# First attention layer of a two-layer network on one core: scores of a head pair interleaved by row halves, value matmuls on 256 queries, a second buffer for V

## The chip, the core and the metric

One core of a Trainium2 chip runs the whole program. The core has five engines that run their own queues and meet at semaphores: TensorE (matmuls and transposes, output into PSUM, eight banks of 512 f32 columns on 128 partitions), VectorE, ScalarE, GpSimd (POOL) and SyncE, which only issues DMAs here. The metric is the time of one execution in microseconds (us); less is better. Data are f32 unless a row says bf16. An f32 matmul instruction shows as two records (PE) and two weight loads (PEld) in the trace, a transpose as one of each.

## The reference, cut to what matters

The network is four residual blocks on x of shape (2, 1024, 128): an attention without projection of its output, a mixture of experts, a second attention with 16 heads, and a two-layer block with local attention. The change touches the first:

```python
    def _L0_attn_ref(x, Wq, Wk, Wv):
        ...
        Q = (x @ Wq.T).reshape(b, n, H, R)
        K = (x @ Wk.T).reshape(b, n, H, R)
        V = (x @ Wv.T).reshape(b, n, H, d)
        attn = jnp.einsum('bnhr,bmhr->bhnm', Q, K)
        attn = jax.nn.softmax(attn, axis=-1)
        out = jnp.einsum('bhnm,bmhd->bnd', attn, V)
        return out
    ...
    x = L0_attn_x
    x = x + _layernorm(_L0_attn_ref(_layernorm(x, axis=-1), L0_attn_Wq, L0_attn_Wk, L0_attn_Wv), axis=-1)
```

With H = 8 heads, R = 64 and d = 128: for each batch half and head, 1024 queries against 1024 keys, a softmax without scale or mask, and the weighted values summed over the heads.

## The kernel before

The first attention runs as four head pairs (`PAIRS`) times two batch halves: eight rounds, each of the same instructions. Heads of a pair lie side by side in the partitions: `q_st` and `k_st` hold head 0 on rows 0-63 and head 1 on rows 64-127; `v_st` holds the values of both, 128 columns each. A round has 16 units (`NU`): unit u is head u // 8 and the block of 128 queries u % 8.

For each unit TensorE makes the scores (`scores`, L557: two matmuls of 64 rows and 512 columns, into the bank pair 2 * (u % 2)), VectorE the negated maximum (L1115), ScalarE the exp with the row sum (L1557), VectorE one over the sum and the normalisation in place (L1120, L1122). TensorE transposes the probabilities by eight 128 x 128 transposes into banks 4 and 5 (`turn`, L572); ScalarE copies bank 4 (L1563) and VectorE bank 5 (L1128) into `probsT`. When the four units of a chunk (512 queries of one head) are there, eight matmuls with the values as weights and 512 columns add them into bank 6 or 7 (`weigh`, L582), two per unit, so that a chunk takes four units. Head 1 adds to what head 0 left in the bank, and VectorE adds the bank to `yT` (L1135).

What sets the order is the code of each engine's loop alone. On TensorE (L597 to L603): scores of u, transposes of u - 2, two value matmuls. The scores of u wait until the exp of u - 2 has freed its two banks. At the end of a round the projections of the next round stand between the last units: q (banks 0 and 1), k (2 and 3), and, last of all, V into banks 0 to 3 (`a_proj_v`), which ScalarE (L1541) and VectorE (L1101) copy into `v_st`. That buffer is single, so the V projection stands behind all value matmuls of the round. Unit 0 of the next round waits for q, k and the first half of V, unit 1 for the second half.

`probs` has four buffers (`NPB`), `probsT` two. GpSimd only copies the next pair's weights (L1785 to L1787). No DMA runs in this stage.

Of the kernel before, what the change touches and what calls it, by code (L numbers as in the profile page):

```python
# [12 lines left out]
P = 128  # L13
# [5 lines left out]
CH = 512  # L19
NCH = TOK // CH  # L20
# [35 lines left out]
def build(nc, a, out):  # L56
    with ExitStack() as ctx:
# [24 lines left out]
        probsT = sb("probsT", [P, 2, QT, CH])  # L82
        negmax = sb("negmax", [P, 2 * STRIP])
# [62 lines left out]
        v_nat = sb("v_nat", [P, TILES, P])  # L146

# [335 lines left out]
        def _(pe):  # L483
# [68 lines left out]
            with pe.Fori(0, PAIRS) as p:  # L552
                for b in range(BATCH):
# [3 lines left out]
                    def scores(u):  # L557
                        r, qt = R0 * (u // QT), u % QT
                        if u == 0:
# [3 lines left out]
                        elif u == 1:  # L563
                            pe.wait_ge(s_a_v1, m + 1)
                        else:
                            pe.wait_ge(s_a_exp, n0 + u - 1)
                        for n in range(2):
                            ins = pe.matmul(ps[:, 2 * (u % 2) + n, :], q_st[r:r + R0, qt * P:(qt + 1) * P],  # L568
                                            k_st[r:r + R0, n * CH:(n + 1) * CH], start=True, stop=True)
                        ins.then_inc(s_a_scores, 1)  # L570
# [11 lines left out]
                    def weigh(c, k0, k1):  # L582

                        head, qc = c // 2, c % 2
                        if k0 == 0:
                            pe.wait_ge(s_a_evA, n0 + 4 * c + 5)
                            pe.wait_ge(s_a_evB, n0 + 4 * c + 5)
                            if head == 0:
                                pe.wait_ge(s_a_oadd, 2 * m + 1)
                        for kt in range(k0, k1):  # L590
                            ins = pe.matmul(ps[:, 6 + qc, :], v_st[:, kt, head * P:(head + 1) * P],  # L591
                                            probsT[:, c % 2, kt, :], start=(head == 0 and kt == 0),
                                            stop=(head == 1 and kt == QT - 1), skip_group_check=True)
                        if head == 1 and k1 == QT:
                            ins.then_inc(s_a_pv, 1)

                    for u in range(NU):  # L597
                        scores(u)
                        if u >= 2:
                            turn(u - 2)  # L600
                        if u >= 6:
                            c, k = (u - 6) // 4, (u - 6) % 4
                            weigh(c, 2 * k, 2 * k + 2)  # L603
# [6 lines left out]
                    weigh(2, 4, 6)  # L610
                    pe.wait_ge(s_a_exp, n0 + NU)
                    a_proj_k(nb)
                    turn(NU - 1)
                    weigh(2, 6, 8)
                    weigh(3, 0, 8)
# [1357 lines left out]
```

## Time and profile before

| | us |
|---|---|
| median of 3 runs | 2117.53 |
| lowest and highest | 2064.26, 2120.01 |
| the profiled execution, its span | 2081.0 |
| TensorE busy in it (matmuls) | 1778.6 |
| VectorE, ScalarE, GpSimd busy | 1214.5, 927.3, 375.6 |

The profiled execution is one of its own and not among the three runs. In the rows below, a time is in us from the start of the span and a mean in ns; "x8" is the number of records in a merged row, and the time of a merged row runs from the start of its first record to the end of its last. Records overlap, since the next matmul begins while the last one still drains; for the pace one reads starts, not lengths. What stands in brackets is the idle time of the engine before the row and what ended it. PEclk or the mean clock is the granted share of 2.4 GHz; each short stretch is at 1.00 or 0.50.

### The profile page before, as it was taken

What the parts mean: (1) busy time and instruction counts of PE and PEld (TensorE: products, weight loads), DVE (VectorE), ACT (ScalarE), POOL (GpSimd) and SP (SyncE); (2) the same over time, 40 slices, a digit from 0 to 9 for tenths busy, and PEclk for the clock granted to TensorE, in tenths of its full rate; (3) what the DMA queues carried; (4) which work ended last, traced back from release to release, by engine and by line L of the source; (5) the groups of instructions that cost most, each with busy time, mean ns of one, the idle gap of its engine ahead of it and who ended that gap; (6) DMA issues with size and microseconds to landing.
All of it is one profiled execution on the core that took longest, in us unless ns stands there. A gap on an engine that the chain in (4) does not pass through costs nothing.

```text
span 2081.0 us, 31701 instructions
## 1 busy us (share of the span) xinstructions
PE 1778.6 (85%) x10724; PEld 954.1 (46%) x10724; DVE 1214.5 (58%) x2711; ACT 927.3 (45%) x2162; POOL 375.6 (18%) x208
## 2 busy tenths in 40 slices
PE   7999999999999879964999989989947886778766
PEld 4454444444544443332544545445524554245543
DVE  6554645546555546673665556546577764467744
ACT  2333423334333223322766657657525564255632
POOL 0000000000000002331000000000017873078820
PEclk8899988999999979985876668678778998889978
DMA  4000000000000000012000000000010000000000
GB/s 106 0 1 0 0 0 0 0 0 0 0 0 0 0 0 0 0 56 86 18 14 14 22 23 11 12 23 2 2 46 1 0 1 1 1 1 0 1 1 20
DMA packets 25961, 24.10 MB, mean 12 GB/s; under 512 B 4834, under 2 KB 19500, under 8 KB 25804
## 3 DMA queue, kind: packets, MB, share of 16 engines
q1 hardware_dynamic: 25836, 22.52, 3.6%
q8 instruction: 68, 1.11, 0.2%
q14 instruction: 57, 0.47, 0.1%
HBM read 18.32 MB, written 4.19 MB: 11 GB/s over the span
## 4 chain that ended last, share of the span: by engine, by line
PE 66%; POOL 12%; DVE 10%; issue 8%; ACT 2%; SPq 1%; DMA 1%; POOLq 0%; DVEq 0%; ACTq 0%
PE ps L568 12%; PE ps L591 11%; PE ps L796 7%; PE ps L578 7%; PE ps L740 5%; PE ps L766 5%; POOL ss L1862 4%; POOL probsT L1873 3%; PE ps L758 2%; DVE arena L1291 2%; PE ps L700 2%; POOL q_st L1860 2%; PE ps L804 2%; PE ps L694 1%; PE ps L541 1%
## 5 line engine op out<-in xcount | busy, mean ns | idle before, releaser
L1291 DVE CUSTOM_DVE_ANT_0 arena<-ps,arena 128x128 f32<-128x128 f32 (+7 forms) x258 | 194.2, 753 | 210.8 <-PE ps L740 161.1
L568 PE MATMUL ps<-k_st,q_st 64*128 64x512 f32 x512 | 269.0, 650 | 6.7 <-ACT probs L1557 6.7
L1115 DVE TENSOR_REDUCE negmax<-ps 128x1 f32<-128x1024 f32 x128 | 156.7, 1224 | 194.8 <-PE ps L568 194.8
L591 PE MATMUL ps<-probsT,v_st 128*128 128x512 f32 x512 | 238.7, 599 | 0.0
L1654 ACT ACTIVATE probs<-arena,negmax 128x128 f32<-128x128 f32 (+7 forms) x258 | 199.8, 775 | 57.9 <-DVE negmax L1294 54.9
L1563 ACT COPY probsT<-ps 128x512 f32<-128x512 f32 x128 | 74.9, 585 | 307.3 <-PE ps L578 307.3
L796 PE MATMUL ps<-ident,probs 128*128 128x128 f32 x832 | 190.6, 355 | 7.6 <-ACT probsT L1680 3.2
L1680 ACT COPY probsT<-ps 128x512 f32<-128x512 f32 (+3 forms) x256 | 127.2, 497 | 132.9 <-PE ps L796 132.2
L1557 ACT ACTIVATE probs<-ps,negmax 128x1024 f32<-128x1024 f32 x128 | 142.6, 1114 | 51.9 <-DVE negmax L1115 50.9
L578 PEld LDWEIGHTS ps<-ident,probs 128*128 128x128 f32 x1024 | 118.0, 147 | 100.8 <-issue 76.1
L796 PEld LDWEIGHTS ps<-ident,probs 128*128 128x128 f32 x832 | 113.9, 175 | 101.0 <-issue 87.3
L568 PEld LDWEIGHTS ps<-k_st,q_st 64*128 64x128 f32 x512 | 90.9, 196 | 149.6 <-issue 81.3
L578 PE MATMUL ps<-ident,probs 128*128 128x128 f32 x1024 | 147.7, 290 | 0.0
L1743 ACT ACTIVATE probsT<-ps,d_nm 128x128 f32<-128x128 f32 x256 | 89.9, 377 | 98.9 <-DVE d_nm L1450 98.9
L766 PE MATMUL ps<-probsT,v_st 128*32 128x128 f32 x2368 | 128.6, 327 | 5.1 <-issue 4.3
L591 PEld LDWEIGHTS ps<-probsT,v_st 128*128 128x128 f32 x512 | 90.9, 193 | 77.6 <-issue 77.6
L1785 POOL COPY wq_st<-w0qk 128x128 f32 (+1 forms) x5 | 1.5, 292 | 633.0 <-PE ps L568 613.4
L882 PE MATMUL ps<-arena 128*128 128x512 f32 x128 | 83.7, 790 | 35.0 <-ACT arena L1759 18.2
L1122 DVE TENSOR_SCALAR probs<-probs,rrow 128x1024 f32<-128x1024 f32 x128 | 96.4, 753 | 4.5
L740 PE MATMUL ps<-k_st,q_st 64*128 64x512 bf16 (+3 forms) x194 | 65.1, 393 | 36.6 <-DMA k_st<-c_parts 25.9
L1128 DVE COPY probsT<-ps 128x512 f32<-128x512 f32 x128 | 87.5, 684 | 14.3 <-PE ps L578 14.3
L1862 POOL TENSOR_TENSOR ss<-ss,half_c 128x16 f32<-128x16 f32 x32 | 93.2, 2912 | 0.4
(243 smaller groups left out, 2969.7 us busy)
## 6 DMA issues: line engine op xcount, KB each, us to landing
c_parts<-arena SPq DMA_DIRECT2D x4, 768.0 KB, 4.3
yT<-c_parts SPq DMA_DIRECT2D x64, 48.0 KB
arena<-in_L_ffn_w_dram SPq DMA_DIRECT2D x3, 512.0 KB
work<-in_L_ffn_wqkv_dram SPq DMA_DIRECT2D x1, 1536.0 KB
q_st<-c_parts SPq DMA_DIRECT2D x32, 48.0 KB
k_st<-c_parts SPq DMA_DIRECT2D x32, 48.0 KB
x_sb<-in_L_attn_x_dram SPq DMA_DIRECT2D x2, 512.0 KB, 4.5
yT<-c_parts SPq DMA_DIRECT2D x32, 32.0 KB
```

The lines of the kernel that those rows point to most:

```text
L568: ins = pe.matmul(ps[:, 2 * (u % 2) + n, :], q_st[r:r + R0, qt * P:(qt + 1) * P], k_st[r:r + R0, n * CH:(n + 1) * CH], start=True, stop=True)
L578: ins = pe.transpose(ps[:, 4 + half, i * P:(i + 1) * P], probs[:, u % NPB, kt * P:(kt + 1) * P], ident[:, :])
L591: ins = pe.matmul(ps[:, 6 + qc, :], v_st[:, kt, head * P:(head + 1) * P], probsT[:, c % 2, kt, :], start=(head == 0 and kt == 0), stop=(he ...
L740: ins = pe.matmul(ps[:, 2 * (u % 2) + n, 0:e - n * CH], c_qs[b][r:r + 64, c, qt * P:(qt + 1) * P], c_ks[b][r:r + 64, c, n * CH:e], start=T ...
L766: ins = pe.matmul(ps[STRIP * j:STRIP * j + STRIP, 6 + qt % 2, 0:P], c_v[:, b, kt, STRIP * j:STRIP * j + STRIP], c_pT[:, qt % 2, j, kt, :], ...
L796: ins = pe.transpose(ps[:, 4, kt * P:(kt + 1) * P], probs[:, u % NPB, kt * P:(kt + 1) * P], ident[:, :])
L1115: dve.tensor_reduce(negmax[:, u:u + 1], s2, AX_X, ALU.max, negate=True)\
L1291: dve.tensor_tensor_reduce(c_sb[:, u % 2, 0:w], s2, c_T[:, j, SEQ - w:SEQ], 1.0, -3.0e38, ALU.add, ALU.max, cmax[:, u:u + 1]).then_inc(s_c ...
L1557: act.activation(probs[:, u % NPB, :], s2, ACT.Exp, bias=negmax[:, u:u + 1], accum_out=rowsum[:, u:u + 1]).then_inc(s_a_exp, 1)
L1654: act.activation(probs[:, u % NPB, 0:w], c_sb[:, u % 2, 0:w], ACT.Exp, bias=negmax[:, u:u + 1], accum_out=rowsum[:, CU * b + u:CU * b + u ...
L1680: act.copy(c_pT[:, qt % 2, j, 0:k, :], ps[:, 4, 0:k * P].rearrange("p (k c) -> p k c", c=P)).then_inc(s_c_evA, 1)
L1862: pool.tensor_tensor(ss[:, par, :], ss[:, par, :], half_c[:, :], ALU.pow).then_inc(s_d_rn, 1)
```

## The change

The three parts of the change are one reordering of a round.

A step i now scores both heads for query block i: four matmuls that alternate between rows 0-63 and 64-127, head 0 into banks 0 and 1, head 1 into banks 2 and 3. Unit u is now query block u // 2 of head u % 2. All four wait until both exps of the step before are done. A chunk is 256 queries (`HC`) of both heads: for each head eight value matmuls with 256 columns, into one half of bank 6 or 7, six of them between the transposes of the two units and two behind. V has two buffers, `v_st` and `v_nat` (`a_v`), used in turn, so the V projection of the next round stands ahead of the last eight value matmuls. VectorE takes both maxima of a step first, then copies and normalisations in turn; ScalarE both exps between its two copies.

```diff
--- before.py
+++ after.py
...
+HC = 256
...
+        a_pT = probsT[:, :, :, :].rearrange("p a k c -> p (a k c)")\
+            .rearrange("p (s n k c) -> p s n k c", s=2, n=2, k=QT)
...
+        a_v = [v_st[:, :, :], v_nat[:, :, :].rearrange("p (k n) c -> p k (n c)", n=2)]
...
-                    def scores(u):
-                        r, qt = R0 * (u // QT), u % QT
-                        if u == 0:
+                    def scores(i):
+
+                        if i == 0:
                             pe.wait_ge(s_a_q, m + 1)
                             pe.wait_ge(s_a_k, m + 1)
                             pe.wait_ge(s_a_v0, m + 1)
-                        elif u == 1:
                             pe.wait_ge(s_a_v1, m + 1)
                         else:
-                            pe.wait_ge(s_a_exp, n0 + u - 1)
+                            pe.wait_ge(s_a_exp, n0 + 2 * i)
                         for n in range(2):
-                            ins = pe.matmul(ps[:, 2 * (u % 2) + n, :], q_st[r:r + R0, qt * P:(qt + 1) * P],
-                                            k_st[r:r + R0, n * CH:(n + 1) * CH], start=True, stop=True)
-                        ins.then_inc(s_a_scores, 1)
+                            for head in range(2):
+                                r = R0 * head
+                                ins = pe.matmul(ps[:, 2 * head + n, :], q_st[r:r + R0, i * P:(i + 1) * P],
+                                                k_st[r:r + R0, n * CH:(n + 1) * CH], start=True, stop=True)
+                                if n == 1:
+                                    ins.then_inc(s_a_scores, 1)
 
                     def turn(u):
                         pe.wait_ge(s_a_norm, n0 + u + 1)
@@ -579,41 +585,45 @@
                                                    probs[:, u % NPB, kt * P:(kt + 1) * P], ident[:, :])
                             ins.then_inc(s_a_trans, 1)
 
-                    def weigh(c, k0, k1):
-
-                        head, qc = c // 2, c % 2
+                    def weigh(c, head, k0, k1):
+
                         if k0 == 0:
-                            pe.wait_ge(s_a_evA, n0 + 4 * c + 5)
-                            pe.wait_ge(s_a_evB, n0 + 4 * c + 5)
-                            if head == 0:
+                            pe.wait_ge(s_a_evA, n0 + 4 * c + head + 4)
+                            pe.wait_ge(s_a_evB, n0 + 4 * c + head + 4)
+                            if c == 0 and head == 0:
                                 pe.wait_ge(s_a_oadd, 2 * m + 1)
                         for kt in range(k0, k1):
-                            ins = pe.matmul(ps[:, 6 + qc, :], v_st[:, kt, head * P:(head + 1) * P],
-                                            probsT[:, c % 2, kt, :], start=(head == 0 and kt == 0),
+                            ins = pe.matmul(ps[:, 6 + c // 2, (c % 2) * HC:(c % 2 + 1) * HC],
+                                            a_v[b][:, kt, head * P:(head + 1) * P],
+                                            a_pT[:, c % 2, head, kt, :], start=(head == 0 and kt == 0),
                                             stop=(head == 1 and kt == QT - 1), skip_group_check=True)
-                        if head == 1 and k1 == QT:
+                        if c % 2 == 1 and head == 1 and k1 == QT:
                             ins.then_inc(s_a_pv, 1)
 
-                    for u in range(NU):
-                        scores(u)
-                        if u >= 2:
-                            turn(u - 2)
-                        if u >= 6:
-                            c, k = (u - 6) // 4, (u - 6) % 4
-                            weigh(c, 2 * k, 2 * k + 2)
+                    for i in range(QT):
+                        scores(i)
+                        if i >= 1:
+                            turn(2 * i - 2)
+                        if i >= 3:
+                            weigh((i - 3) // 2, (i - 3) % 2, 0, 6)
+                        if i >= 1:
+                            turn(2 * i - 1)
+                        if i >= 3:
+                            weigh((i - 3) // 2, (i - 3) % 2, 6, 8)
                     nb = 1 - b
                     if b == 1:
                         pe.wait_ge(s_a_wst, p + 2)
                     pe.wait_ge(s_a_exp, n0 + NU - 1)
                     a_proj_q(nb)
                     turn(NU - 2)
-                    weigh(2, 4, 6)
+                    weigh(2, 1, 0, 6)
+                    turn(NU - 1)
+                    weigh(2, 1, 6, 8)
                     pe.wait_ge(s_a_exp, n0 + NU)
                     a_proj_k(nb)
-                    turn(NU - 1)
-                    weigh(2, 6, 8)
-                    weigh(3, 0, 8)
+                    weigh(3, 0, 0, 8)
                     a_proj_v(nb, m + 2)
+                    weigh(3, 1, 0, 8)
...
-                    for u in range(NU):
+                    for i in range(QT):
+                        u = 2 * i
                         rowmax(u)
-                        if u >= 1:
-                            rrecip(u - 1)
-                        if u >= 2:
+                        rowmax(u + 1)
+                        if i >= 1:
                             copy_out(u - 2)
-                    rrecip(NU - 1)
+                        rrecip(u)
+                        if i >= 1:
+                            copy_out(u - 1)
+                        rrecip(u + 1)
                     copy_out(NU - 2)
-                    a_evac_k(m + 2)
                     copy_out(NU - 1)
                     add_out(0)
+                    a_evac_k(m + 2)
+                    a_evac_v(m + 2, 1 - b)
                     add_out(1)
-                    a_evac_v(m + 2)
...
-                    for u in range(NU):
-                        if u >= 2:
+                    for i in range(QT):
+                        u = 2 * i
+                        if i >= 1:
                             copy_out(u - 2)
                         soft(u)
+                        soft(u + 1)
+                        if i >= 1:
+                            copy_out(u - 1)
+                    a_evac_q(m + 2)
                     copy_out(NU - 2)
-                    a_evac_q(m + 2)
                     copy_out(NU - 1)
-                    a_evac_v(m + 2)
+                    a_evac_v(m + 2, 1 - b)
```

Three places show it in the order of the instructions. First TensorE in the middle of a round. Before: scores, transposes of a unit, two value matmuls, twice over for two units (L568 scores, L578 transposes, L591 values, L566 the next wait's value):

```order
L566 REGISTER_ALU
L568 MATMUL ps<-k_st,q_st 128x512 x2
L578 MATMUL ps<-ident,probs 128x128 x8
L591 MATMUL ps<-probsT,v_st 128x512 x2
L566 REGISTER_ALU
L568 MATMUL ps<-k_st,q_st 128x512 x2
L578 MATMUL ps<-ident,probs 128x128 x8
L591 MATMUL ps<-probsT,v_st 128x512 x2
```

The changed kernel at the same place, one step (L573 scores, L584 transposes, L596 values):

```order
L569 REGISTER_ALU
L573 MATMUL ps<-k_st,q_st 128x512 x4
L579 REGISTER_ALU
L584 MATMUL ps<-ident,probs 128x128 x8
L596 MATMUL ps<-probsT,v_st 128x256 x6
L584 MATMUL ps<-ident,probs 128x128 x8
L596 MATMUL ps<-probsT,v_st 128x256 x2
```

The scores of two units now stand together, the value matmuls are eight of 256 columns instead of four of 512, and six of them part the transposes of the two units.

Second, TensorE at the end of a round, before (L523, L529, L541 are the projections of q, k and V for the next round):

```order
L523 MATMUL ps<-xT,wq_st 128x512 x2
L578 MATMUL ps<-ident,probs 128x128 x8
L591 MATMUL ps<-probsT,v_st 128x512 x2
L611 REGISTER_ALU
L529 MATMUL ps<-xT,wk_st 128x512 x2
L578 MATMUL ps<-ident,probs 128x128 x8
L591 MATMUL ps<-probsT,v_st 128x512 x2
L586 REGISTER_ALU
L591 MATMUL ps<-probsT,v_st 128x512 x8
L534 REGISTER_ALU
L541 MATMUL ps<-wv_st,xT 128x256 x8
L568 MATMUL ps<-k_st,q_st 128x512 x6
```

And of the change (L527, L533 and L545 are the projections):

```order
L527 MATMUL ps<-xT,wq_st 128x512 x2
L584 MATMUL ps<-ident,probs 128x128 x8
L596 MATMUL ps<-probsT,v_st 128x256 x6
L579 REGISTER_ALU
L584 MATMUL ps<-ident,probs 128x128 x8
L596 MATMUL ps<-probsT,v_st 128x256 x2
L533 MATMUL ps<-xT,wk_st 128x512 x2
L596 MATMUL ps<-probsT,v_st 128x256 x8
L538 REGISTER_ALU
L545 MATMUL ps<-wv_st,xT 128x256 x8
L591 REGISTER_ALU
L596 MATMUL ps<-probsT,v_st 128x256 x8
```

The V projection has moved ahead of the last eight value matmuls, and the k projection behind the transposes of the last unit.

Third, VectorE in the middle of a round, before, one unit (L1115 maximum, L1120 and L1122 normalisation, L1128 copy of transposed probabilities, L1113 and L1126 wait values):

```order
L1113 REGISTER_ALU
L1115 TENSOR_REDUCE negmax<-ps 128x1
L1120 RECIPROCAL rrow<-rowsum 128x1
L1122 TENSOR_SCALAR probs<-probs,rrow 128x1024
L1126 ISA
L1128 COPY probsT<-ps 128x4x128
```

And of the change, one step of two units:

```order
L1123 REGISTER_ALU
L1125 TENSOR_REDUCE negmax<-ps 128x1 [waits s_a_scores]
L1123 REGISTER_ALU
L1125 TENSOR_REDUCE negmax<-ps 128x1 [waits s_a_scores]
L1136 ISA
L1138 COPY probsT<-ps 128x4x128 [waits s_a_trans]
L1130 RECIPROCAL rrow<-rowsum 128x1 [waits s_a_exp]
L1132 TENSOR_SCALAR probs<-probs,rrow 128x1024 [waits s_a_rrow]
L1136 ISA
L1138 COPY probsT<-ps 128x4x128 [waits s_a_trans]
L1130 RECIPROCAL rrow<-rowsum 128x1 [waits s_a_exp]
L1132 TENSOR_SCALAR probs<-probs,rrow 128x1024 [waits s_a_rrow]
```

The work is the same for two units; both maxima come first, and each copy stands ahead of a normalisation.

## Rows read from the trace of the kernel before

**Rows 1.** The page: busy time, share of the span, instructions of each engine.
```profile
PE 1778.6 (85%) x10724; PEld 954.1 (46%) x10724; DVE 1214.5 (58%) x2711; ACT 927.3 (45%) x2162; POOL 375.6 (18%) x208
```

**Rows 2.** Stretch, length, busy PE, PEld, DVE, ACT, POOL, clock, DMA: the rounds.
```profile
33.24:129.68 96.44, 95.60 (x281) 46.44 (x280) 46.25 (x68) 30.09 (x50) 0.00 (x0) 0.84 0.00 1
...
211.42:293.16 81.74, 80.90 (x281) 40.03 (x281) 46.25 (x68) 30.56 (x50) 0.00 (x0) 1.00 0.00 0
293.16:388.17 95.01, 94.17 (x275) 45.65 (x275) 46.26 (x68) 29.26 (x50) 0.87 (x3) 0.84 0.00 0
...
sum 683.76, PE 676.68 PEld 333.25 DVE 370.37 ACT 244.60 POOL 3.49; mean PE 84.58 PEld 41.66 DVE 46.30 ACT 30.58 POOL 0.44
```

**Rows 3.** Order in time, one unit mid-round: start, length, engine, line, operation, tiles.
```profile
87.48 1.98 PE L568 MATMUL ps<-k_st,q_st 64*128 64x512 f32 x4
89.39 1.09 PE L578 MATMUL ps<-ident,probs 128*128 128x128 f32 x8
89.50 1.22 DVE L1115 TENSOR_REDUCE negmax<-ps 128x1 f32<-128x1024 f32 x1 [1.97 <-PE ps L568]
90.32 1.88 PE L591 MATMUL ps<-probsT,v_st 128*128 128x512 f32 x4
...
90.83 0.75 DVE L1122 TENSOR_SCALAR probs<-probs,rrow 128x1024 f32<-128x1024 f32 x1
90.83 1.11 ACT L1557 ACTIVATE probs<-ps,negmax 128x1024 f32<-128x1024 f32 x1 [0.17 <-DVE negmax L1115]
...
91.49 0.68 DVE L1128 COPY probsT<-ps 128x512 f32<-128x512 f32 x1
...
92.13 0.69 PE L568 MATMUL ps<-k_st,q_st 64*128 64x512 f32 x1
```

**Rows 4.** TensorE in order, the opening of the third round, then of the fourth.
```profile
215.96 1.98 PE L568 MATMUL ps<-k_st,q_st 64*128 64x512 f32 x4 [0.84 <-ACT probs L1557]
...
218.89 1.98 PE L568 MATMUL ps<-k_st,q_st 64*128 64x512 f32 x4
...
301.40 1.97 PE L578 MATMUL ps<-ident,probs 128*128 128x128 f32 x8
303.30 3.78 PE L568 MATMUL ps<-k_st,q_st 64*128 64x512 f32 x4
```

**Rows 5.** TensorE in order, the tail of the first round.
```profile
110.65 1.88 PE L523 MATMUL ps<-xT,wq_st 128*128 128x512 f32 x4
...
112.37 1.04 PE L578 MATMUL ps<-ident,probs 128*128 128x128 f32 x8
...
116.68 1.04 PE L578 MATMUL ps<-ident,probs 128*128 128x128 f32 x8
...
117.55 8.75 PE L591 MATMUL ps<-probsT,v_st 128*128 128x512 f32 x20
...
126.14 3.62 PE L541 MATMUL ps<-wv_st,xT 128*128 128x256 f32 x16
```

**Rows 6.** TensorE, scores of the last attention: first two of 48 records, and the next.
```profile
1647.89 0.27 PE L931 MATMUL ps<-probsT 64*64 64x64 f32 x1
1647.90 0.32 PE L935 MATMUL ps<-probsT 64*64 64x128 f32 x1
...
1649.06 1.16 PE L946 MATMUL ps<-probsT,arena 128*128 128x128 f32 x8
```

**Rows 7.** Busy time by stretch around changes of the clock, columns as in rows 2.
```profile
297.90:328.60 30.70, 30.70 (x64) 14.64 (x64) 14.27 (x23) 9.66 (x17) 0.00 (x0) 0.50 0.00 0
328.60:388.00 59.40, 59.40 (x203) 29.22 (x203) 28.54 (x43) 18.22 (x31) 0.00 (x0) 1.00 0.00 0
24.80:28.00 3.20, 3.20 (x12) 1.63 (x11) 3.17 (x9) 0.58 (x1) 0.00 (x0) 1.00 0.00 0
21.40:24.80 3.40, 3.40 (x18) 3.40 (x18) 2.91 (x6) 0.00 (x0) 0.00 (x0) 0.54 0.39 130
```

**Rows 8.** TensorE in order, what it did up to 25.29, in the last two of these.
```profile
20.16 5.13 PE L518 MATMUL ps<-ident,arena 128*128 128x128 f32 x30 [2.42 <-DVE w0v L1070]
```

More of the change, by code:

```diff
@@ L1097, in a_evac_k, with a_evac_v @@
                 dve.tensor_copy(k_st[:, :].rearrange("p (n c) -> p n c", n=2), ps[:, 2:4, :]).then_inc(s_a_k, 1)
-            def a_evac_v(m):
+            def a_evac_v(m, b):
                 dve.wait_ge(s_a_projv1, m)
-                dve.tensor_copy(v_st[:, 4:8, :].rearrange("p (n k) c -> p n (k c)", n=2),
+                dve.tensor_copy(a_v[b][:, 4:8, :].rearrange("p (n k) c -> p n (k c)", n=2),
                                 ps[:, 2:4, :]).then_inc(s_a_v1, 1)
             a_evac_k(1)
-            a_evac_v(1)
+            a_evac_v(1, 0)
             dve.wait_ge(s_a_ozero, 1)
@@ L1126, in copy_out @@
                         dve.wait_ge(s_a_trans, 2 * (n0 + u) + 2)
-                        c, q = u // 4, (u % 4) * P
-                        dve.tensor_copy(probsT[:, c % 2, 4:8, q:q + P],
+                        c, q = u // 4, (u // 2 % 2) * P
+                        dve.tensor_copy(a_pT[:, c % 2, u % 2, 4:8, q:q + P],
                                         ps[:, 5, :].rearrange("p (k c) -> p k c", k=4)).then_inc(s_a_evB, 1)
@@ L1537, in a_evac_q, with a_evac_v @@
                 act.copy(q_st[:, :].rearrange("p (n c) -> p n c", n=2), ps[:, 0:2, :]).then_inc(s_a_q, 1)
-            def a_evac_v(m):
+            def a_evac_v(m, b):
                 act.wait_ge(s_a_projv0, m)
-                act.copy(v_st[:, 0:4, :].rearrange("p (n k) c -> p n (k c)", n=2), ps[:, 0:2, :]).then_inc(s_a_v0, 1)
+                act.copy(a_v[b][:, 0:4, :].rearrange("p (n k) c -> p n (k c)", n=2), ps[:, 0:2, :])\
+                   .then_inc(s_a_v0, 1)
             act.activation(sd[:, 0:1], eps_c[:, 0:1], ACT.Exp)
             a_evac_q(1)
-            a_evac_v(1)
+            a_evac_v(1, 0)
             with act.Fori(0, PAIRS) as p:
@@ L1561, in copy_out @@
                         act.wait_ge(s_a_trans, 2 * (n0 + u) + 1)
-                        c, q = u // 4, (u % 4) * P
-                        act.copy(probsT[:, c % 2, 0:4, q:q + P],
+                        c, q = u // 4, (u // 2 % 2) * P
+                        act.copy(a_pT[:, c % 2, u % 2, 0:4, q:q + P],
                                  ps[:, 4, :].rearrange("p (k c) -> p k c", k=4)).then_inc(s_a_evA, 1)
-                    for u in range(NU):
-                        if u >= 2:
+                    for i in range(QT):
+                        u = 2 * i
+                        if i >= 1:
                             copy_out(u - 2)
                         soft(u)
+                        soft(u + 1)
+                        if i >= 1:
+                            copy_out(u - 1)
+                    a_evac_q(m + 2)
                     copy_out(NU - 2)
-                    a_evac_q(m + 2)
                     copy_out(NU - 1)
-                    a_evac_v(m + 2)
+                    a_evac_v(m + 2, 1 - b)
             norm_out(0)
```

## Prediction

> **What bounds the kernel now.** I read the page first: TensorE is busy for 85% of the span, VectorE for 58%, ScalarE for 45% [rows 1]. An average says nothing of a stage, so I then cut the first attention layer at its eight rounds, one for each head pair and batch half [rows 2]. The reader is to see that matmuls are busy for nearly all of each round (80.90 of 81.74 us) while VectorE needs 46.25 and ScalarE 30.56, and that two of the eight rounds took 96.44 and 95.01 us, those with a mean clock of 0.84. The stage is 683.8 of 2081.0 us; the other 1397.2 us hold no line of the change.
>
> The order in time shows what a unit (one head, one block of 128 queries) costs in the middle of a round [rows 3]: scores begin at 87.48, transposes at 89.39, value matmuls at 90.32, the next scores at 92.13. That is 1.91 + 0.93 + 1.81 = 4.65 us without a gap, so matmuls set the pace. The release chain behind the scores is short of that: maximum at 89.50 (1.22), exp at 90.83, and scores could follow 1.30 behind an exp's start. A round now is 4.54 for its first two units, four times 2.93 for those without value matmuls [rows 4], ten times 4.65, and a tail of 19.03 from the query projection at 110.65 to the next round at 129.68 [rows 2, 5]: 81.8, as measured.
>
> **Scores of a pair.** The number of score instructions stays, two for each unit. What changes is that consecutive ones sit on rows 0-63 and 64-127, in different banks. Nothing in this stage shows two 64-row matmuls at once. Another stage does [rows 6]: for one tile of the last attention, 48 records, 16 each of 64, 64 and 128 columns, begin at 1647.89, and the next operation at 1649.06. One at a time they would take 4096 columns x 0.84 ns = 3.4 us, where 0.84 ns is 8.59 us over 20 x 512 columns [rows 5]; side by side in columns alone, 1.7 us. They took 1.17. So f32 matmuls on different rows did run together, and wrote the same partitions of two banks. I therefore take four instructions for the price of two: 1.91 us for a pair instead of 3.82. The bounds are 1.91 (full overlap) and 3.82 (none); 1.91 is nearest to the row.
>
> The Trainium skill, "TensorE: Matmul & The Clock Gate", Part 3, says that matmuls start and end strictly in program order. Row and rule differ: in [rows 6] a record of L935 begins 0.01 us after the first of L931, though four records of L931 and L933 on the same array rows stand ahead of it in the code. By the rule the pair would cost one record more, 0.43 us.
>
> **Transposes** stay eight to a unit: 0.93 us mid-round, 0.87 in the tail.
>
> **Value matmuls on 256 queries.** Twice the instructions with half the columns. The value projection has that shape: 16 records in 3.54 us, or 0.221 each, its weight loads hidden under them [rows 5]; for 512 columns 8.59 / 20 = 0.43. So two heads' worth for one pair, 16 records, is 3.54 against 2 x 1.72: +0.1. Below this the bound is 3.44, two of the old; above, nothing in the rows.
>
> **The chain behind a pair.** Scores of pair i+1 now need both exps of pair i, since four banks hold one pair. From the start of the scores: 2.02 to the first maximum, 1.22, 1.22 for the second, 0.11 to its exp, 1.30 from there to the next scores: 5.87 us [rows 3]. Where value matmuls run, TensorE has 0.93 + 2.65 (12 records) + 0.93 + 0.89 (4 records) = 5.40 to do behind its scores and the chain needs 3.96: hidden. VectorE, by the same rows, with 0.9 for a normalisation and 0.68 for a copy, counted from the end of the scores: two maxima to 2.5, copy of unit 2i-2 to 3.2, normalisation of 2i to 4.1, copy of 2i-1 to 5.3 (its transposes end at 4.5), normalisation of 2i+1 to 6.2, ahead of the next maximum at 7.4. ScalarE has less. The order of the queues costs nothing there. If matmuls fell below the chain, 5.87 would be the floor for a pair.
>
> Steady pair: 1.91 + 0.93 + 2.65 + 0.93 + 0.89 + 0.09 (hand-over, 1.81 less 1.72) = 7.40, against 9.30. Five in a round: 37.0.
> Opening: pairs 0 to 2 have no value matmuls, so the chain shows: 3 x 5.87 = 17.6, against 16.3 for the first six units. The loss is all in pair 0, where the second unit's scores used to cover the first one's maximum: a gap of about 4 us instead of 0.84 [rows 4].
> Tail: 1.72 (q) + 0.87 + 2.65 + 0.87 + 0.89 + 1.72 (k) + 3 x 3.54 (values, V projection, values) = 19.3, against 19.03.
> Round: 73.9, against 81.74; eight rounds 591.2.
>
> **V double-buffered** lets the V projection go ahead of the last value matmuls. It hides the copies of V out of PSUM (1024 columns, as many as a maximum reads in 1.22 us) behind 3.54 us of work. But they are hidden now too: V's last record ends at 129.76 and the next round's scores began at 129.68 [rows 2, 5]. I give it nothing. With the cover gone, as ahead of the first round, all scores wait for the upper half of V, where now only unit 1 does: 1.22 + 0.2 = 1.4 us, once. The last sum into `yT`, 512 columns like the copy of 0.68 [rows 3], runs under the next scores.
>
> **Clock.** Where it fell, the 0.84 us gap behind 64-row scores came first: granted 1.00 in the whole round to 293.16 [rows 2], 0.50 (1.2 GHz) from 297.9 to 328.6, while scores and transposes alone ran without a pause, and 1.00 (2.4 GHz) again after value matmuls [rows 7]. At the low level the scores of a unit took 3.7 us and its transposes 1.9 [rows 4]. The fourfold gap of the change is likelier to bring the drop, in every round. But then two heads on all 128 rows follow, not one on 64, and dense full-row work was followed by the high level. I take one pair scored at the low level a round: 3.8 - 1.9 = 1.9, eight times: 15. Bounds: 0 (no drop), and low until the value matmuls have run: 3 pairs x 1.9, 0.95 for transposes, 2.6 for twelve value records: 9.2 a round, 73. The two long rounds of before, 14.7 and 13.3, go with it.
>
> Here the Trainium skill speaks against the change, same page, Part 4: transposes do not engage the full clock. Then a round's opening, transposes in large part, would stay low, the bound of 73. The trace speaks otherwise: from 21.4 to 24.8 TensorE did only the transposes of L518 at 0.54, and from 24.8 it was granted 1.00 [rows 7, 8].
>
> **Sum.** 591.2 + 15.0 + 1.4 = 607.6, against 683.8: 76 less. 2081.0 - 76.2 = 2005. The profiled execution lies 36 below the median of the three runs, 2117.53, which spread over 56 us. Two more long rounds at 14 would explain most of that, and the change removes their cause or makes it alike in all; I add nothing and predict **2005 us**.
>
> **Rivals.**
> 1. *Strict order of starts*: overlap of neighbours only, 64 pairs x 0.43 = 27 more: 2032. For: only the rule. Against: the starts in [rows 6]. 12%.
> 2. *The clock stays low until value matmuls* in every round: 2005 - 15 + 73 = 2063. For: [rows 7], 30.7 us low over uninterrupted scores. Against: those were on 64 rows. 15%.
> 3. *No drop at all*: 1990. Against: the longer gap. 8%.
> 4. *Slower: the pair does not overlap*, although the rows differ. Opening 3 x 7.78, steady 5 x 9.31, tail 19.3: 89.2 a round, 713.6; and 64-row scores behind a 4 us gap keep the clock low as in [rows 7], 14 a round, 112. That is 827 against 683.8: 2224. It decides if less than a third of the 1.91 is overlapped (76 / 64 = 1.19 of 1.91 can be lost, with the clock as forecast). Against: [rows 6]. This is also the case that the change does not do what it says. 7%.
> The forecast itself: 58%, with its own range 1990 to 2025.
>
> **How the numbers follow.** Range 1975 to 2068: from rival 3 less 15 for the unchanged stages, whose clock differs from run to run, to rival 2 plus 5. About 2% is what a measurement can tell from no change; 2% under 2117.5 is 2075. The forecast and rivals 1 to 3 lie below it, but a median of before nearer to the profile would put rival 2 inside 2%: faster 86%, same 7%, slower 7%.
>
> **What would show it.** Score rows of a pair, 8 records, in about 2 us; steady pairs 7.4 us apart; opening pairs 5.9 apart, with TensorE waiting for the second exp; rounds of 74 to 77, all alike; a short stretch at 0.50 early in each round. Wrong if 8 score records take 3.7 us, if rounds contain 0.50 until the value matmuls, or if steady pairs wait for VectorE.

## The result and the profile after

The changed kernel took 2003.24 us in the median of four runs (1989.09 to 2017.10), the kernel before 2105.41 in the median of its four (2064.26 to 2120.01). The ratio is 0.9637, 95% interval 0.9533 to 0.9740: faster. It leaves out two slow runs of the kernel before (2117.53 and 2120.01), so that 2003 stands against the 2079 of the other two. The forecast was 2005 us, range 1975 to 2068.

The profiled execution had a span of 2006.2 us against 2081.0. First the page of the changed kernel, busy time by engine:

```profile
PE 1664.6 (83%) x11236; PEld 1013.2 (51%) x11236; DVE 1217.6 (61%) x2711; ACT 921.7 (46%) x2162; POOL 375.8 (19%) x208
```

TensorE lost 114 us of busy time against [rows 1]; VectorE and ScalarE kept theirs within 6 us. Next the stretches (columns as in [rows 2]): three of the eight rounds of the changed kernel, and all that follows them:

```profile
34.70:108.75 74.05, 67.56 (x346) 47.98 (x346) 45.63 (x68) 29.72 (x50) 0.00 (x0) 0.98 0.00 1
108.75:183.23 74.48, 68.79 (x346) 48.76 (x346) 46.16 (x69) 29.64 (x50) 0.88 (x3) 0.95 0.00 1
183.23:258.96 75.73, 69.20 (x346) 48.41 (x346) 46.17 (x69) 29.72 (x50) 0.00 (x0) 0.95 0.00 0
633.60:2006.20 1372.60, 1095.11 (x8398) 610.28 (x8397) 825.96 (x2092) 675.55 (x1751) 371.19 (x189) 0.80 0.04 13
```

The later rounds repeat 74.5 and 75.7 in turn. From the first scores at 34.45 to the end of the last value matmul at 633.65 the stage took 599.2 us; before, it took 683.4 from the first scores to the end of the last V projection at 716.61 ([rows 2] cut it a little later, at 717): 84.2 less. What follows took 1372.6, against this row of before:

```profile
717.00:2081.00 1364.00, 1082.94 (x8397) 606.34 (x8397) 822.33 (x2092) 675.22 (x1752) 371.03 (x189) 0.81 0.04 14
```

That part has the same instructions in both and cost about 8 us more this time.

One round of the changed kernel in TensorE's order, from the opening into the steady part and then the tail (the answer to [rows 3], [rows 4] and [rows 5]):

```profile
108.50 1.99 PE L573 MATMUL ps<-k_st,q_st 64*128 64x512 f32 x8
114.16 3.79 PE L573 MATMUL ps<-k_st,q_st 64*128 64x512 f32 x8 [3.68 <-ACT probs L1571]
117.88 2.77 PE L584 MATMUL ps<-ident,probs 128*128 128x128 f32 x12
120.99 0.66 PE L584 MATMUL ps<-ident,probs 128*128 128x128 f32 x4 [0.34 <-DVE probsT L1138]
121.87 1.99 PE L573 MATMUL ps<-k_st,q_st 64*128 64x512 f32 x8 [0.23 <-ACT probs L1571]
...
134.89 1.99 PE L573 MATMUL ps<-k_st,q_st 64*128 64x512 f32 x8
136.81 1.09 PE L584 MATMUL ps<-ident,probs 128*128 128x128 f32 x8
137.74 2.76 PE L596 MATMUL ps<-probsT,v_nat 128*128 128x256 f32 x12
140.33 1.04 PE L584 MATMUL ps<-ident,probs 128*128 128x128 f32 x8
141.20 1.03 PE L596 MATMUL ps<-probsT,v_nat 128*128 128x256 f32 x4
142.16 1.99 PE L573 MATMUL ps<-k_st,q_st 64*128 64x512 f32 x8
...
163.89 1.88 PE L527 MATMUL ps<-xT,wq_st 128*128 128x512 f32 x4
...
175.98 3.62 PE L545 MATMUL ps<-wv_st,xT 128*128 128x256 f32 x16
179.44 3.62 PE L596 MATMUL ps<-probsT,v_nat 128*128 128x256 f32 x16
```

Eight score records, two heads, take 1.99 us, as long as the four of one head did before. Steady steps stand 7.27 us apart (134.89 to 142.16). In the opening TensorE idles 3.68 us until the second exp is done, and the scores behind it take 3.79 instead of 1.99. The granted clock around that place, in stretches of the changed kernel:

```profile
108.50:113.70 5.20, 1.99 (x9) 0.69 (x8) 3.70 (x5) 1.93 (x3) 0.88 (x3) 0.98 0.01 2
113.70:120.50 6.80, 6.34 (x20) 3.43 (x20) 3.70 (x6) 1.88 (x4) 0.00 (x0) 0.51 0.00 0
120.60:188.80 68.20, 62.51 (x327) 45.48 (x326) 42.80 (x65) 28.07 (x49) 0.00 (x0) 1.00 0.00 1
```

The clock fell to 1.2 GHz in the idle stretch, for 6.8 us, and was back at 2.4 GHz well before the first value matmuls of the round at 130.47. Rounds 3, 5 and 7, those of 75.7 us, have two stretches of 3.4 us at 0.50 instead, one over the scores of step 1 and one over those of step 3 (188.6 and 202.2 in the third round); the first round has only one, over step 3.

### The profile page after: what moved, and what is told of

Its sections match the earlier page's. It is cut to its first block, busy times and chain, and to the rows that moved or that the text cites. A ratio compares the mean times of both kernels' runs of the same rounds, so it can differ in the third digit from the quotient of the medians.

```text
span 2006.2 us, 32765 instructions
## 1 busy us (share of the span) xinstructions
PE 1664.6 (83%) x11236; PEld 1013.2 (51%) x11236; DVE 1217.6 (61%) x2711; ACT 921.7 (46%) x2162; POOL 375.8 (19%) x208
## 4 chain that ended last, share of the span: by engine, by line
PE 61%; POOL 12%; DVE 11%; issue 10%; ACT 3%; SPq 1%; DMA 1%; POOLq 0%; DVEq 0%; ACTq 0%
PE ps L596 11%; PE ps L806 7%; PE ps L573 7%; PE ps L750 5%; PE ps L776 5%; PE ps L584 5%; POOL ss L1880 4%; POOL probsT L1891 3%; PE ps L768 2%; PE ps L710 2%; DVE arena L1304 2%; PE ps L814 2%; POOL q_st L1878 2%; PE ps L704 2%; PE ps L545 1%
## 5 line engine op out<-in xcount | busy, mean ns | idle before, releaser
L1125 DVE TENSOR_REDUCE negmax<-ps 128x1 f32<-128x1024 f32 x128 | 150.8, 1220 | 83.9 <-PE ps L573 83.9
L573 PE MATMUL ps<-k_st,q_st 64*128 64x512 f32 x512 | 144.5, 688 | 32.2 <-ACT probs L1571 30.3
L584 PEld LDWEIGHTS ps<-ident,probs 128*128 128x128 f32 x1024 | 118.9, 145 | 84.7 <-issue 52.9
L584 PE MATMUL ps<-ident,probs 128*128 128x128 f32 x1024 | 145.2, 284 | 18.1 <-DVE probsT L1138 14.1
L596 PE MATMUL ps<-probsT,v_st 128*128 128x256 f32 x512 | 119.8, 379 | 0.0
L596 PE MATMUL ps<-probsT,v_nat 128*128 128x256 f32 x512 | 119.8, 379 | 0.0
L750 PE MATMUL ps<-k_st,q_st 64*128 64x512 bf16 (+3 forms) x194 | 71.1, 429 | 37.2 <-DMA k_st<-c_parts 26.4
L596 PEld LDWEIGHTS ps<-probsT,v_st 128*128 128x128 f32 x512 | 93.5, 190 | 12.4 <-issue 1.9
L596 PEld LDWEIGHTS ps<-probsT,v_nat 128*128 128x128 f32 x512 | 93.5, 190 | 12.4 <-issue 1.9
```

The costliest lines, as they stand in the source:

```text
L573: ins = pe.matmul(ps[:, 2 * head + n, :], q_st[r:r + R0, i * P:(i + 1) * P], k_st[r:r + R0, n * CH:(n + 1) * CH], start=True, stop=True)
L584: ins = pe.transpose(ps[:, 4 + half, i * P:(i + 1) * P], probs[:, u % NPB, kt * P:(kt + 1) * P], ident[:, :])
L596: ins = pe.matmul(ps[:, 6 + c // 2, (c % 2) * HC:(c % 2 + 1) * HC], a_v[b][:, kt, head * P:(head + 1) * P], a_pT[:, c % 2, head, kt, :], s ...
L750: ins = pe.matmul(ps[:, 2 * (u % 2) + n, 0:e - n * CH], c_qs[b][r:r + 64, c, qt * P:(qt + 1) * P], c_ks[b][r:r + 64, c, n * CH:e], start=T ...
L1125: dve.tensor_reduce(negmax[:, u:u + 1], s2, AX_X, ALU.max, negate=True)\
```

## Experiments

The theory after the result: most of the gain is two heads' score matmuls running at once on different rows; 256-column value matmuls cost nothing; V's second buffer is worth little; the long idle stretch in the opening now costs a short low clock in each round.

**No overlap.** The changed kernel with all four score matmuls of a step on the rows of head 0; it leaves out the scores of head 1:

```diff
-                                r = R0 * head
+                                r = 0
```

> All four score matmuls of a step take rows 0-63 of q_st and k_st, so the scores of head 1 are left out (head 0's are computed twice); nothing else differs from the changed kernel. Overlap by rows: the eight score records of a step, 1.99 us in the changed kernel, take 3.7 us at the high clock; a steady step goes from 7.27 to 9.0, an opening step from 5.7 to 7.5, a round from 75 to at least 87, and if the clock then stays at 1.2 GHz until the value matmuls, as in two rounds of before, to about 101. Time 2100 to 2215. Rival (the gain of the change came from fewer switches between 64-row and 128-row work, not from overlap): about 2003.

Measured: 2122.81 us, ratio 1.0197 to the kernel before, interval 1.0139 to 1.0256. A steady step and a round of this kernel, in TensorE's order and as a stretch:

```profile
148.56 3.70 PE L573 MATMUL ps<-k_st,q_st 64*128 64x512 f32 x8 [0.63 <-ACT probs L1571]
152.19 1.09 PE L584 MATMUL ps<-ident,probs 128*128 128x128 f32 x8
```

```profile
212.72:304.51 91.79, 88.72 (x345) 57.58 (x345) 47.38 (x69) 28.82 (x50) 0.00 (x0) 0.89 0.00 0
304.51:393.48 88.97, 84.86 (x345) 55.71 (x345) 47.10 (x69) 28.82 (x50) 0.87 (x3) 0.92 0.00 0
```

The score records go back to 3.70 us, a steady step to 8.98 (148.56 to 157.54), a round to 88 to 97. The rest of the change by itself is thus a loss of about 2% against before (1.4 to 2.6% by the interval), and the overlap is worth about 120 us here: the stage took 722.2 us in this trace against 599.2. That includes what the clock cost, which was at 0.50 for 123 us of this stage and for 51 of the changed kernel's. It is the forecast's rival 4, and its price was set too high: 2224. Rounds were to be 89.2 at the high clock plus 14; they were 90.5 on average over the seven whose starts are seen. Both parts were too large. A steady step took 8.98 and not 9.31, and opening steps at the high clock 6.52 to 7.17 and not 7.78, so that a round at the high clock would have been about 85 (an estimate from these steps and the tail of 19.1). And the clock was low for 10.2 us in four of the eight rounds and for 13.7 to 30.7 in the others, not for 30.7 in all.

**Does the alternation matter?** The same four matmuls, head 0 twice, then head 1 twice:

```diff
-                        for n in range(2):
-                            for head in range(2):
+                        for head in range(2):
+                            for n in range(2):
```

> The four score matmuls of a step in the order head 0, head 0, head 1, head 1 in place of alternating. If a matmul on free rows may start past one that waits for busy rows: the eight records stay at 2.0 to 2.1 us, the round at 75, the time at 2003. By strict program order of starts: four records of head 0 one after another, the first of head 1 beside the last of them, seven slots of 0.43 us, 3.1 us a step, 1.1 more; 64 steps, 70 us, and time about 2075.

Measured: 1997.14 us (2003.83 and 1990.45), no different from the changed kernel's 2003.24. In TensorE's order:

```profile
142.26 1.99 PE L573 MATMUL ps<-k_st,q_st 64*128 64x512 f32 x8
144.19 1.09 PE L584 MATMUL ps<-ident,probs 128*128 128x128 f32 x8
145.12 2.76 PE L596 MATMUL ps<-probsT,v_nat 128*128 128x256 f32 x12
```

Still 1.99 us, where strict order would make it about 3.1. The records start two by two, 0.013 us apart (142.261 and 142.274, then 142.794 and 142.808), against 0.006 us when the heads alternate. So a matmul on free rows starts ahead of one that stands before it and waits for busy rows. The Trainium skill, "TensorE: Matmul & The Clock Gate", Part 3, states strict program order for starts; on these rows the trace disagrees. What matters is that both heads stand together, not that they alternate.

**V in one buffer.**

```diff
-        a_v = [v_st[:, :, :], v_nat[:, :, :].rearrange("p (k n) c -> p k (n c)", n=2)]
+        a_v = [v_st[:, :, :], v_st[:, :, :]]
...
-                    a_proj_v(nb, m + 2)
                     weigh(3, 1, 0, 8)
+                    a_proj_v(nb, m + 2)
...
-                    a_evac_v(m + 2, 1 - b)
                     add_out(1)
+                    a_evac_v(m + 2, 1 - b)
```

> V in one buffer again (v_st), its projection behind all value matmuls of the round, the rest as in the changed kernel. My theory after the forecast: the second buffer is worth the copy of V's upper half, since all scores of step 0 wait for it: 0.1 + 1.22 + 0.1 = 1.4 us a round of TensorE idle ahead of the scores, eight times 1.4 = 11 us, 2014. Rival (the copies are hidden without the second buffer, as they were before the change): 2003. The gap ahead of the first scores of a round tells them apart; a difference of 11 us in the time lies within the spread of runs.

Measured: 2010.31 us (2007.31 and 2013.31). The first scores of a round and one whole round:

```profile
185.20 1.99 PE L573 MATMUL ps<-k_st,q_st 64*128 64x512 f32 x8 [1.41 <-DVE v_st L1111]
190.84 1.85 PE L573 MATMUL ps<-k_st,q_st 64*128 64x512 f32 x6 [3.65 <-ACT probs L1571]
```

```profile
110.48:185.45 74.97, 67.64 (x346) 48.19 (x346) 46.17 (x68) 29.62 (x50) 0.87 (x3) 0.98 0.00 1
```

The gap of 1.41 us is there, in the place and of the size expected. Yet the rounds averaged 75.1 us against 75.0 in the changed kernel: the mean clock of the round is 0.98 instead of 0.95, since the clock was low for 3.4 us in seven of the eight rounds and not for 6.8. So the second buffer takes away the wait, and nearly all of that was given back to the clock. Whether the wait itself shortened the low stretch, no run tells. The 11 us that I expected are not shown; its worth in this kernel lies below what these runs can tell.

**The kernel before, profiled again.**

> The kernel before, unchanged, profiled once more. The first profile had two rounds of the first attention 13 to 15 us longer, with half the clock for 30.7 us each. If that is what makes its runs differ (2064 to 2120 us), the span follows the number of such rounds: 1398 for the rest, 82 for a short round and 96 for a long one, so 2052 plus 14 for each. Rival: the rest of the kernel makes the difference, and the number of long rounds does not track the span.

Measured: span 2087.2 us. Its one long round, a short one, and all that follows the stage:

```profile
197.09:293.57 96.48, 95.64 (x281) 46.61 (x281) 46.27 (x69) 30.07 (x50) 0.00 (x0) 0.84 0.00 0
115.35:197.09 81.74, 80.90 (x281) 40.03 (x281) 46.28 (x69) 30.56 (x50) 0.87 (x3) 1.00 0.00 1
703.00:2087.20 1384.20, 1103.15 (x8397) 616.05 (x8397) 824.57 (x2092) 675.46 (x1751) 371.10 (x189) 0.79 0.04 13
```

One long round instead of two, and a longer span all the same. The rest took 20 us more than in the first profile, with a clock of 0.79 against 0.81. The formula 2052 plus 14 a round gives 2066; it fails. Long rounds are real, 14.7 us each, but between these two profiles the rest of the kernel made the larger difference, 20 us. It also means that the gain in the stage depends on which profile of before is taken: 84.2 us against the first, 69.5 against this one (668.7).

**Keeping the clock up in the opening.** Work without use behind the scores of step 0, first as matmuls, then as transposes:

```diff
                     for i in range(QT):
+                        if i == 1:
+                            pe.wait_ge(s_a_evA, n0 + 1)
+                            for k in range(4):
+                                pe.matmul(ps[:, 4, :], ident[:, :], k_st[:, 0:CH], start=True, stop=True)
                         scores(i)
```

> Four full-row matmuls of 512 columns (identity times keys, into bank 4, never read) behind the scores of step 0 of each round, where the changed kernel stands idle for 3.68 us; nothing else. They take 3.4 us and fit into the idle time. Clock theory: without the idle stretch the granted clock stays at 1.00 ahead of step 1, whose scores go from 3.8 to 1.99 us; a round goes from 75.0 to about 73, the time from 2003 to about 1988. Rival (the low stretch comes from the 64-row scores or at a fixed point of a round, whatever stands ahead): rounds stay at 75 and step 1 stays slow.

Measured: 1965.28 us (1955.13 and 1975.43). The opening, and one round:

```profile
107.30 1.99 PE L573 MATMUL ps<-k_st,q_st 64*128 64x512 f32 x8
109.21 3.70 PE L607 MATMUL ps<-k_st,ident 128*128 128x512 f32 x8
112.96 1.99 PE L573 MATMUL ps<-k_st,q_st 64*128 64x512 f32 x8
```

```profile
326.50:398.94 72.44, 69.55 (x354) 48.74 (x354) 46.16 (x69) 29.84 (x50) 0.00 (x0) 1.00 0.00 0
616.00:1953.30 1337.30, 1059.74 (x8398) 595.14 (x8397) 823.65 (x2092) 674.57 (x1751) 371.14 (x189) 0.82 0.04 14
```

The scores of step 1 take 1.99 us, the clock stays at 1.00, and six of the seven rounds whose length is seen take 72.4 (one 74.1, with 3.4 us at 0.50 in step 3), on average 72.7 against 75.0. That is 2.3 a round or 18 us. The medians lie 38 us apart, and the two profiles 53: what goes beyond 18 lies in the rest of the kernel, 1337 us in this profile against 1373, where nothing was changed. So this run shows 18 us for the clock, not 38. (Beside this run and the next three, the kernel before took 2105.11 us in the median, beside the changed kernel 2105.41.)

The transposes: `range(32)` and `pe.transpose` of 128 x 128 blocks of `k_st` in place of the matmul.

> As the run before, but with 32 transposes of 128 x 128 (3.4 us) in place of the four matmuls. By the rows (the clock rose behind the transposes of L518): the same as with matmuls, rounds of about 73 and 1988 us. By the Trainium skill, TensorE: Matmul & The Clock Gate, Part 4 (transposes do not engage the full clock): the clock falls as if nothing stood there, rounds of 75, step 1 at 3.8 us, 2003 us.

Measured: 1994.92 us (1992.51 and 1997.34). The openings of the second and the seventh round:

```profile
109.30 3.71 PE L607 MATMUL ps<-ident,k_st 128*128 128x128 f32 x32
113.04 1.99 PE L573 MATMUL ps<-k_st,q_st 64*128 64x512 f32 x8
```

```profile
479.65 1.52 PE L573 MATMUL ps<-k_st,q_st 64*128 64x512 f32 x5
482.42 1.12 PE L573 MATMUL ps<-k_st,q_st 64*128 64x512 f32 x3 [1.24 <-issue]
483.47 3.71 PE L607 MATMUL ps<-ident,k_st 128*128 128x128 f32 x32
487.12 1.99 PE L573 MATMUL ps<-k_st,q_st 64*128 64x512 f32 x8
```

Behind 3.7 us of transposes alone the scores of step 1 run at the high clock in all eight rounds, as behind matmuls. So transposes held the clock up here, as [rows 7, 8] had said, and the Trainium skill, "TensorE: Matmul & The Clock Gate", Part 4, by which they would not, does not hold for these f32 transposes. The first rounds took 72.4 and 72.9, the later ones 74.2 to 76.3. Two things were new in them. The clock was at 0.50 for 3.4 us in rounds 4, 5 and 6 (from 272.5, 334.0 and 422.7; at 334.0 it fell during the transposes, behind a pause). And the first scores of rounds 3, 5 and 7 have a pause of 1.66, 1.65 and 1.24 us that no semaphore explains. Those three rounds are the ones behind a jump back of the loop, which holds two rounds. This trace also has packets of the queue that brings instructions all through the stage; from 185 to 540 us:

```profile
q8 instruction: 21, 0.34, 0.4%
```

In the same stretch the changed kernel and the kernel with four matmuls have none. One such packet starts 0.6 to 1.1 us ahead of each of the three pauses (180.61, 330.08 and 480.04). Instructions of the loop, which has 64 more transposes, are thus brought in again in every pass, and the pauses go with that; no run isolates it as their cause.

**Real work in the gap.** The last eight value matmuls of a round go behind the first scores of the next; VectorE's sum of bank 7 follows them. A table names the matmuls of step i as (head, first, end); the first round of all has none, and a block behind the loop issues those of the last:

```diff
+            OPEN = {0: [(1, 0, 8)]}
...
                 for i in range(QT):
                     scores(i)
                     if i >= 1:
                         turn(2 * i - 2)
+                    if i in OPEN and not first:
+                        for head, k0, k1 in OPEN[i]:
+                            weigh(3, head, k0, k1, 1)
...
                 weigh(3, 0, 0, 8)
                 a_proj_v(nb, m + 2)
-                weigh(3, 1, 0, 8)
```

> The last eight value matmuls of a round (chunk 3, head 1) stand behind the scores of step 0 of the next round, and VectorE adds bank 7 to yT after the normalisations of step 0; the last round's stand behind the loop. Real work of 3.5 us takes the idle stretch of 3.68. Theory: seven rounds lose 3.5 us of tail and the low clock of step 1 (1.9): 69.6 us a round, 38 less in all, about 1965 us. Rival (the opening is bound by something the values push back, such as VectorE's sum of 0.69 us ahead of the next maximum): the opening grows by what the tail loses, about 2003.

Measured: 1976.38 us (1964.09 to 1984.44, four runs), ratio 0.9514, interval 0.9395 to 0.9632. The opening of the third round:

```profile
178.72 1.99 PE L576 MATMUL ps<-k_st,q_st 64*128 64x512 f32 x8 [1.41 <-DVE v_st L1132]
180.64 3.72 PE L599 MATMUL ps<-probsT,v_nat 128*128 128x256 f32 x16
184.36 1.99 PE L576 MATMUL ps<-k_st,q_st 64*128 64x512 f32 x8
```

The values fit into the gap and the clock stays up there. Rounds took 72.1 at first, with 3.4 us at 0.50 in step 3, and 70.4 later, not 69.6: I had forgotten what the moved matmuls had covered, V's copy, and 1.41 us came back as a wait. The last version leaves three matmuls behind the V projection for that and spreads thirteen over steps 0, 1 and 2 (eight, three, two); VectorE's sum moves to step 2:

```diff
-            OPEN = {0: [(1, 0, 8)]}
+            OPEN = {0: [(0, 3, 8), (1, 0, 3)], 1: [(1, 3, 6)], 2: [(1, 6, 8)]}
...
-                weigh(3, 0, 0, 8)
                 a_proj_v(nb, m + 2)
+                weigh(3, 0, 0, 3)
```

> Thirteen of the last sixteen value matmuls of a round deferred: eight behind the scores of step 0 of the next round, three in step 1, two in step 2; three stay behind the V projection to cover its copies. Theory: the tail shrinks by 5.7 us and the opening stays at 5.7 us a step, since steps 1 and 2 have 1.4 us idle each; with the clock high, about 67 us a round, 55 less in all, about 1948 us. Rival (the transposes of steps 1 and 2, which wait for copies, are pushed behind the values and delay the next scores): no better than eight deferred, about 1965.

Measured: 1952.55 us (1942.78 to 1958.63, four runs), ratio 0.9406, interval 0.9315 to 0.9497. A round:

```profile
236.88:303.87 66.99, 65.82 (x346) 47.26 (x346) 45.97 (x68) 29.77 (x50) 0.88 (x3) 1.00 0.00 0
```

Matmuls are busy for 65.8 of 67.0 us at 1.00, in six of the seven rounds seen. It computes the whole network and beats both kernels: 50.7 us below the median of the changed kernel, and the intervals of their ratios to before (0.9315 to 0.9497, 0.9533 to 0.9740) do not meet. The stage took 542.2 us against 599.2. The short round of 81.74 in [rows 2] has become 67.0.

**What the long rounds of before come from.** One full-row matmul in the 0.84 us gap of the kernel before:

```diff
                     for u in range(NU):
+                        if u == 2:
+                            pe.wait_ge(s_a_evA, n0 + 1)
+                            pe.matmul(ps[:, 4, :], ident[:, :], k_st[:, 0:CH], start=True, stop=True)
                         scores(u)
```

> The kernel before with one full-row matmul of 512 columns (never read) in the 0.84 us gap ahead of the scores of unit 2, 0.86 us of work. Clock theory: no round is long any more; all eight take 81.8 us, the stage ends at about 688, 1 to 2 long rounds of 14.7 us less than before: 14 to 29 us off the span, which the rest of the kernel (it ran 1364 and 1385 us in the two profiles of before) may hide or double. Rival (long rounds start from something else, such as the 64-row scores themselves): one or two rounds of 96 us remain.

Measured: 2065.53 us (2061.31 and 2069.76), ratio 0.9827, interval 0.9656 to 0.9998, so the gain is hardly clear of nothing. The stage and the rest, and behind them the low stretch in the second profile of before, with the scores that it starts in:

```profile
34.00:690.00 656.00, 654.62 (x2256) 322.31 (x2255) 370.89 (x545) 246.00 (x401) 3.51 (x12) 1.00 0.00 0
690.00:2059.50 1369.50, 1085.13 (x8397) 607.81 (x8397) 821.63 (x2091) 675.73 (x1751) 371.40 (x189) 0.80 0.04 14
```

```profile
201.40:232.10 30.70, 30.70 (x64) 14.82 (x64) 14.45 (x23) 9.66 (x17) 0.00 (x0) 0.50 0.00 0
201.37 3.76 PE L568 MATMUL ps<-k_st,q_st 64*128 64x512 f32 x4 [0.84 <-ACT probs L1557]
```

The seven rounds whose length is seen take 81.89 us, and the clock is at 1.00 in the whole stage. Two things speak for the 0.84 us gap, not 64-row scores as such, as the start of a long round. All three long rounds of the two profiles of before begin within 0.5 us of the end of that gap (38.2, 297.6 and 201.4), and with the gap filled none began. The second is weak by itself: at three long rounds in sixteen, none in eight would come about by chance one time in five (an estimate). So the gap is the likely start, and not shown to be.

## Why the prediction was right, point by point

- **Scores of a pair, 1.91 us.** Right: 1.92 from the start of the scores to the transposes (134.89 to 136.81). The reading of another stage's 48 records carried over. Without overlap the same kernel is slower than before.
- **Value matmuls on 256 queries.** Right: 3.45 us for 16 records (172.53 to 175.98) against 3.54 forecast, which had been read up to the next scores, and 3.44 for the old shape. Steady step 7.27 against 7.40.
- **The chain in the opening, 5.87 us.** Right in kind: 5.66 at the high clock (107.30 to 112.96 with matmuls in the gap). The two maxima end 2.36 us after the first begins, not 2.44; the second exp follows at once, not after 0.11; and the scores start 1.25 us behind it, not 1.30.
- **VectorE's order costs nothing in steady steps.** Right: no steady step has a wait of TensorE.
- **Tail, 19.3.** 163.89 to 182.98 is 19.1. With these, a round at the high clock was 72.4, forecast 73.9.
- **Clock.** The place and the mechanism were right, the size small: 75.0 less 72.7 or 72.4 is 2.3 to 2.5 us a round against 1.9. What was left out is the transposes of step 0, which ran at the low level too, and in rounds 3, 5 and 7 the second stretch of 3.4 us, over the scores of step 3.
- **V's second buffer, nothing.** The value was about right, the argument half of it. "They are hidden now too" holds for a kernel whose first unit needs only half of V. With both heads scored at once and one buffer, the wait of 1.41 us is there, and the clock gave it back. The 1.4 us once, ahead of the first round, came as forecast.
- **The sum.** Stage 84.2 us shorter, forecast 76.2; the rest of the kernel, forecast as unchanged, 8 longer. That the forecast came within 2 us of the median owes something to these two having opposite signs. The 84.2 are eight times 9.3 (81.74 less 72.4) for the shorter round, plus 29.4 for the two long rounds of this profile, less 20 for the low clock in the opening. The 29.4 were partly luck of the profile chosen: the second one has a single long round. That nothing was added for the 36 us between the profile and the median of before was right for another reason than the one given: the two runs that the ratio keeps have a median of 2079, beside the profile's 2081.
- **What was wrong**: "Two more long rounds at 14 would explain most of that", on the distance of the profile from the median. The second profile of before had fewer long rounds and a longer span. More of what differs from profile to profile is in the stages that the change does not touch. From the end of the first attention's last matmul they took 1364 and 1385 us in the two of before, 1371 with the gap of before filled, 1373 in the changed kernel, 1337 in the one with four matmuls, 1364 to 1380 in the other six. They go with their mean clock, 0.82 in the shortest and 0.79 in the longest of before. Two slips changed little: the second long round was also 96.43 us long, not 95.01 (it was cut at 388.17, and the next scores begin at 389.59), and rival 4 decides if less than 38% of the 1.91 overlaps (0.72 of 1.91), not a third.
- **The rivals.** Strict order (2032) fell by the 1.92 us of a pair and by the grouped run. The low clock until the value matmuls (2063) fell by the stretch from 120.60 on at 1.00. No drop (1990) fell by the 0.50 in every round; filling the gap shows that it would have been worth 18 us. No overlap (2224) did not happen, and made on purpose costs 2123.

## What to carry to other kernels

Where a matmul uses half the rows, put two on different halves next to each other and, as here, into different banks; it halved the time of 64-row f32 scores, and the order between them did not matter. Banks that both heads need at once turn a two-stage pipeline into a gap at the start of each round: look for work of the round before that can stand there, and ask what that work covered where it stood. A gap in TensorE's work can cost more than its own length through the clock that falls with it (here 2.3 to 2.5 us a round on top of 3.68 us idle, and likely 14.7 behind a gap of 0.84), so read the granted clock beside each wait. And before a gain of 20 us in a kernel of 2000 is believed, look where in the trace it lies: the untouched rest alone moved by up to 48 us between profiles.

## What the hardware did that was not expected

- Scores on 64 rows and their transposes, without a pause, did not bring the clock back for 30.7 us in [rows 7], while two heads at once on all 128 rows had it back after 3.4 to 6.8 us, and transposes alone after 3.4. In the kernel with both heads on the same rows, the low stretch lasted between 10.2 and 30.7 us, so 64-row work does not fix its length. A gap of 0.84 us behind 64-row work was followed by a long round in one or two of eight cases; with a full-row matmul in it, in none of eight.
- A pause of 1.24 to 1.66 us in the middle of the first scores of a round, in three of eight rounds, each behind a jump back of the loop, when 32 more transposes stood in each round. No semaphore and no engine released it. Instruction packets ran in every pass of that loop, one shortly ahead of each pause, and none in the changed kernel's from 185 us on; that fetching them was the cause is likely, and not tested.
